# A transformer block on one Trainium2 core: feed-forward product a slot later, window values as a difference, gate product in strips

## The chip, the cores and the metric

The kernel runs on one core of a Trainium2 chip. Its engines run their own instruction streams beside each other: TensorE (PE in the profile, with its weight loads as PEld), VectorE (DVE), ScalarE (ACT), GpSimd (POOL) and SyncE (SP), which here only issues DMAs. They meet through semaphores. The metric is the device time of one execution in microseconds (us).

## The reference

Eight batches of 1024 tokens, 512 wide, go through one block: a modulated layer norm, attention with 16 heads of 32 that adds three parts under a learned gate, a residual, a second modulated layer norm, and a feed-forward part with six routed pairs of rank-16 matrices.

```python
h = _layernorm(x) * (1 + ca) + sa
# attention of h:
q, k, v = _rope(x @ Wq, HD), _rope(x @ Wk, HD), x @ Wv
ck, cv = (blocks of 16 tokens of k and v, weighted by wk_comp, wv_comp)
out_comp = softmax(q ck^T * SCALE, blocks that are over) @ cv
out_sel  = softmax(q k_sel^T * SCALE, causal) @ v_sel       # 2 x 8 tokens of the best 2 blocks
wmask = (cols <= rows) & (cols > rows - WIN)                # WIN = 128
out_win  = softmax(q k^T * SCALE, wmask) @ v
g = softmax(x @ Wg + bg)                                    # 3 gates
out = g0 * out_comp + g1 * out_sel + g2 * out_win
x = x + ga * (out @ Wo + bo)
h = _layernorm(x) * (1 + cb) + sb
# feed-forward of h: top 2 of 6 experts, renormalised weights
x = x + gb * (h @ base_W^T + base_b + (h @ shared_A^T) @ shared_B^T
              + sum_e w_e * (h @ routed_A[e]^T) @ routed_B[e]^T)
```

## The kernel before, in words

A batch is eight tiles of 128 tokens. A token attends in the window part to its own tile and the one before, so a query has 128 keys: for key column j either that of the tile before or its own tile's.

**Stages.** Eight "heads" project batch 0. Then come, for each of seven batches, a first slot, six common slots (`slot`, s = 2 to 7) and a turn; an epilogue (`end_first`, `end_slot`, `last`) finishes batch 7. A slot s does three things at once: attention of tile s of batch b; the output product, residual, second norm, router and feed-forward of tile t = s − 1; and norm, Q, K, V and gate of tile t of batch b + 1. The first slot has attention of tile 1 and the output part of tile 0, and the turn has attention of tile 0 of the next batch and the output part of tile 7, and with them the blocks' compression and the selection.

**What sets the order.** Nothing is scheduled by a program. Each engine's stream is written out by hand in these functions, one list of calls for each engine. Products that end in the two PSUM banks `ps_m` take them in the order of tables (`SLOT_ORDER` and its like, units Q, K, V, QT, KT transposes, G gate, HT, Y output product, H2T, Z router and rank-16 product, F feed-forward, ZT): a unit may begin when the one before it in its bank is read out (`m_free_at`), and its reader waits for `m_full`. Window scores are in `ps_s`, transposed probabilities in `ps_t`, attention values in `ps_o`.

**Precision.** Long products are three fp32r products: hi x hi, lo x hi, hi x lo (L558 to L560 for Q, K, V; L729, L730, L738 for the output; L773, L774, L782 for the feed-forward). Short ones are plain fp32: the gate (`gate_logits`, L579: four chunks of 128x128 tokens as weights against 3 columns), the rank-16 product down (L755) and up (`feed_up`, L790, weights 113 rows).

**Window probabilities.** Scores (L647), VectorE's merge of the two tiles' scores into 128 columns by the mask `later` and the maximum (L1791, L1796), ScalarE's exponentials and normalisation (L1182, L1192), TensorE's transposition of four heads into `ps_t` (L660), two masked copies by VectorE (`split_probs`): `pT_prev` (L1817) for the keys of the tile before, `pT_own` (L1819) for the tile's own keys; the two masks complement each other. Then the values (`window_values`, L685): 16 matmuls in four 32-column strips, `pT_prev` x `v_s[t-1]` and `pT_own` x `v_s[t]`. For tile 0 eight bf16 matmuls with zero open the bank (L695), and only `pT_own` counts.

**Compressed and selected part.** Scores L636, VectorE L1828 to L1856, transposition L679, ScalarE copies it to `pT_cs` (L1219), values L715. The value rows are the tile `csv`; when few blocks are seen, several heads' products run in different rows of TensorE, and so `csv` is replicated by DMA at the start of a batch's first slot: `cv_two` (two copies of 64 rows, L463) and `cv_four` (four of 32 rows, L465), used for tiles 2 and 3, and 0 and 1.

**Other lines that are named.** Residual and norm statistics on VectorE: L1866, L1869, L1718. Rope of Q or K on VectorE (L1758, L1763), then its sum on GpSimd (L1462). The final sum of the block on VectorE (`final`, L1920, L1922), and the store of `xc` by ScalarE's queue. SyncE loads the rows of `x` and the three gate rows `gbc` of a batch in the turn.

## Time and profile before

| | us |
|---|---|
| three runs, median (lowest, highest) | 2219.99 (2219.48, 2226.52) |
| the profiled execution | 2229.21 |
| its span | 2227.3 |
| TensorE busy in it | 2023.9 (91%) |
| VectorE busy | 1793.5 (81%) |
| ScalarE busy | 1327.9 (60%) |
| GpSimd busy | 878.8 (39%) |
| mean granted TensorE clock | 0.967 of full |

The page gives these and the shares of forty slices. Below it, the table of stretches gives each engine's busy time in a stretch, the rows in order of time give each group's start and length with, in brackets, how long the engine was idle before it and which event ended that. Matmul lengths overlap in these rows; the distance between two starts is what a group costs.

### The profile page before, as it was taken

What the parts mean: (1) busy time and instruction counts of PE and PEld (TensorE: products, weight loads), DVE (VectorE), ACT (ScalarE), POOL (GpSimd) and SP (SyncE); (2) the same over time, 40 slices, a digit from 0 to 9 for tenths busy, and PEclk for the clock granted to TensorE, in tenths of its full rate; (3) what the DMA queues carried; (4) which work ended last, traced back from release to release, by engine and by line L of the source; (5) the groups of instructions that cost most, each with busy time, mean ns of one, the idle gap of its engine ahead of it and who ended that gap; (6) DMA issues with size and microseconds to landing.
All of it is one profiled execution on the core that took longest, in us unless ns stands there. A gap on an engine that the chain in (4) does not pass through costs nothing.

```text
span 2227.3 us, 49222 instructions
## 1 busy us (share of the span) xinstructions
PE 2023.9 (91%) x18028; PEld 1465.2 (66%) x18028; DVE 1793.5 (81%) x4806; ACT 1327.9 (60%) x4658; POOL 878.8 (39%) x843
## 2 busy tenths in 40 slices
PE   6988999899999999989999999999999999987876
PEld 3656667666676766667666666766766676665554
DVE  4668888878987888878897788878898788886775
ACT  2346666556665666655666566655666566655654
POOL 1534444334442444334443344434444344432232
PEclk9999999999999999989999999999999999997888
DMA  6210100101011010110001001010001100010000
GB/s 215 63 44 20 30 25 29 44 25 30 20 34 44 20 30 25 33 40 25 25 25 53 15 30 30 30 39 25 29 20 34 44 25 25 29 32 23 20 20 20
DMA packets 43537, 77.56 MB, mean 35 GB/s; under 512 B 7314, under 2 KB 7314, under 8 KB 43299
## 3 DMA queue, kind: packets, MB, share of 16 engines
q1 hardware_dynamic: 32034, 56.85, 8.9%
q10 hardware_dynamic: 11264, 17.57, 2.1%
q8 instruction: 145, 2.38, 0.4%
q14 instruction: 94, 0.76, 0.1%
HBM read 53.38 MB, written 16.83 MB: 32 GB/s over the span
## 4 chain that ended last, share of the span: by engine, by line
PE 51%; DVE 34%; ACT 6%; issue 5%; POOL 2%; DMA 1%; SPq 1%; DVEq 0%; ACTq 0%; POOLq 0%
DVE ps_s L1791 6%; PE ps_o L685 5%; PE ps_t L660 5%; DVE wmax L1796 4%; PE ps_o L715 4%; PE ps_m L558 3%; PE ps_m L560 3%; PE ps_m L559 3%; PE ps_s L679 3%; PE ps_m L755 3%; PE ps_m L773 3%; PE ps_m L774 3%; PE ps_m L782 3%; PE ps_s L636 3%; PE ps_m L790 2%
## 5 line engine op out<-in xcount | busy, mean ns | idle before, releaser
L1182 ACT ACTIVATE pw<-ps_s,wmax 128x128 f32<-128x128 f32 x1024 | 359.3, 380 | 229.6 <-DVE wmax L1796 227.8
L558 PE MATMUL ps_m<-w_hi,h_hi 128*128 128x512 f32 x768 | 340.8, 444 | 8.6 <-DVE h_lo L1927 4.8
L1192 ACT ACTIVATE pw<-pw,wden 128x128 f32<-128x128 f32 x1024 | 313.7, 400 | 30.5 <-DVE wden L1806 30.5
L560 PE MATMUL ps_m<-w_hi,h_lo 128*128 128x512 f32 x768 | 303.2, 395 | 0.0
L559 PE MATMUL ps_m<-w_lo,h_hi 128*128 128x512 f32 x768 | 302.4, 394 | 0.0
L1182 ACT ACTIVATION_READ_ACCUMULATOR pw<-ps_s,wmax 128x1 f32 x1024 | 225.5, 220 | 0.0
L1817 DVE COPY_PREDICATED pT<-keep_prev,ps_t 128x512 f32<-128x512 uint32 x224 | 166.0, 741 | 68.9 <-PE ps_t L660 68.4
L1478 POOL TENSOR_TENSOR css<-css,cden 128x256 f32<-128x256 f32 (+7 forms) x128 | 123.1, 982 | 207.0 <-DVE cden L1856 207.0
L558 PEld LDWEIGHTS ps_m<-w_hi,h_hi 128*128 128x128 f32 x768 | 145.3, 189 | 71.7 <-issue 44.3
L1819 DVE COPY_PREDICATED pT<-keep_own,ps_t 128x512 f32<-128x512 uint32 x256 | 185.3, 724 | 1.0 <-issue 0.3
L685 PE MATMUL ps_o<-pT,v_s 128*32 128x128 f32 x3840 | 168.3, 283 | 13.8 <-DVE pT L1817 8.9
L660 PE MATMUL ps_t<-cst,pw 128*128 128x128 f32 x1024 | 168.3, 290 | 11.4 <-ACT pw L1192 10.4
L647 PE MATMUL ps_s<-kT,qT 32*128 32x256 f32 (+1 forms) x2048 | 144.0, 396 | 29.2 <-ACT pw L1182 21.3
L559 PEld LDWEIGHTS ps_m<-w_lo,h_hi 128*128 128x128 f32 x768 | 145.8, 190 | 34.4 <-issue 11.8
L1505 POOL TENSOR_TENSOR h_lo<-hT,h_hi 128x512 fp32r<-128x512 f32 x57 | 72.8, 1277 | 242.2 <-ACT h_hi L1144 242.2
L560 PEld LDWEIGHTS ps_m<-w_hi,h_lo 128*128 128x128 f32 x768 | 145.1, 189 | 33.8
L1796 DVE TENSOR_REDUCE wmax<-ps_s 128x4 f32<-128x512 f32 x256 | 163.9, 681 | 0.0
L660 PEld LDWEIGHTS ps_t<-cst,pw 128*128 128x128 f32 x1024 | 122.4, 148 | 53.5 <-issue 44.0
L1828 DVE TENSOR_TENSOR css<-ps_s,csmask 128x384 f32<-128x384 f32 (+3 forms) x64 | 65.5, 1024 | 109.9 <-PE ps_s L636 109.7
L1791 DVE COPY_PREDICATED ps_s<-later,ps_s 128x512 f32<-128x512 uint32 x224 | 144.1, 688 | 5.7 <-PE ps_s L647 5.5
L1470 POOL TENSOR_TENSOR css<-css,cm 128x256 f32<-128x256 f32 (+7 forms) x128 | 111.1, 889 | 88.5 <-DVE cm L1841 86.5
L685 PEld LDWEIGHTS ps_o<-pT,v_s 128*32 128x32 f32 x3840 | 93.5, 110 | 79.6 <-issue 44.1
(213 smaller groups left out, 4791.4 us busy)
## 6 DMA issues: line engine op xcount, KB each, us to landing
xa<-x_in SPq DMA_DIRECT2D x65, 256.0 KB, 2.7
xc<-x_in SPq DMA_DIRECT2D x64, 256.0 KB, 2.7
out<-xc ACTq DMA_DIRECT2D x64, 256.0 KB, 2.0
gbc<-gate_rows SPq DMA_DIRECT2D x24, 256.0 KB, 3.4
pw<-wmod_in SPq DMA_DIRECT2D x3, 1024.0 KB, 8.2
pT<-wmod_in SPq DMA_DIRECT2D x3, 1024.0 KB, 7.2
qT<-wqkv_in SPq DMA_DIRECT2D x2, 1024.0 KB, 13.6
cv_two<-csv SPq DMA_DIRECT2D x16, 128.0 KB, 3.1
```

Of the source, the lines that this page charges most:

```text
L558: pe_.matmul(ps[:], h_hi[:, c, :], w_hi[:, col, c, :], start=(c == 0), stop=False)
L559: pe_.matmul(ps[:], h_hi[:, c, :], w_lo[:, col, c, :], start=False, stop=False)
L560: mm = pe_.matmul(ps[:], h_lo[:, c, :], w_hi[:, col, c, :], start=False, stop=(c == NC - 1))
L647: mm = pe_.matmul(ps_s[:, j, (i + 1) * 2 * P - n:(i + 1) * 2 * P], qT[rows, c, t * P:(t + 1) * P], kT[rows, c, k0:k0 + n], start=True, sto ...
L660: mm = pe_.transpose(ps_t[:, j, :], pw[:, head_column(half, j, i), :], ident)
L685: mm = pe_.matmul(ps_o[HD * j:HD * j + HD, c, :], src[0:rows, cols], probs[0:rows, j, :], start=start, stop=stop, skip_group_check=True)
L1182: ins = act.activation(pw[:, hw, :], ps_w[:, j, i, 1, :], ACT.Exp, bias=wmax[:, hw:hw + 1], accum_out=wden[:, 0, hw:hw + 1])
L1192: act.activation(pw[:, hw, :], pw[:, hw, :], ACT.Copy, scale=wden[:, 2, hw:hw + 1]).then_inc(wn_ok, 1)
L1791: dve.copy_predicated(own, later[:].unsqueeze(1).unsqueeze(1).broadcast_to([P, 2, 2, P]), former).then_inc(merged, 1)
L1796: dve.tensor_reduce(wmax[:, h0:h0 + 4].rearrange("p (j i) -> p j i", j=2), ps_w[:, 2 * p:2 * p + 2, :, 1, :], AX.X, ALU.max, negate=True). ...
L1817: dve.copy_predicated(pT_prev[:, g % 2], keep_prev[:].unsqueeze(1).broadcast_to([P, 4, P]), ps_t[:]).then_inc(tw_done, 1)
L1819: dve.copy_predicated(pT_own[:, g % 2], keep_own[:].unsqueeze(1).broadcast_to([P, 4, P]), ps_t[:]).then_inc(tw_done, 1 if t else 2)
```

## The change

1. **Feed-forward a slot later.** The product F of a tile, its rank-16 part (ZT, `feed_up`), `final` and the store move into the slot of the next tile, in front of the output product. The first call of all has nothing to do and only passes the semaphores on; `last` has the units F2 and ZT2 for the last tile. The residual `x1` has two buffers. SyncE loads gate row 1 in slot 2, once F of the tile before has used the old one.
2. **Value difference.** ScalarE copies the whole of `ps_t` to `pT_all`, and this copy frees `ps_t`. VectorE's masked copy to `pT_own` reads `pT_all`, and none is made to a `pT_prev`. GpSimd computes `vd = v_s[t] - v_s[t-1]`, and the values are `pT_all` x `v_s[t-1]` + `pT_own` x `vd`. Tile 0 uses `pT_all` x `v_s[0]` alone, without zero matmuls.
3. **Gate strips.** Four matmuls with 128x32 weights (`wg_w`) against `hT` in four column strips, a copy by ScalarE (`gs`), and one matmul that adds the four and gives 3 columns (unit G2).
4. **Split rank product.** `feed_up` is three fp32r matmuls; VectorE computes the low part of `zT` (`lower_z`).
5. **One replicated tile.** `cv_rep` takes the place of `cv_two` and `cv_four`: four 32-row copies first, the two 64-row ones in slot 2.
6. **Other order.** All engines' lists and the bank tables are written anew.

```diff
-SLOT_ORDER = [("Y", 1), ("Q", 0), ("K", 1), ("QT", 0), ("G", 0), ("H2T", 0), ("Z", 0), ("KT", 1),
-              ("F", 0), ("ZT", 1), ("V", 1), ("HT", 0)]
+SLOT_ORDER = [("F", 0), ("ZT", 1), ("Y", 1), ("Q", 0), ("K", 1), ("QT", 0), ("G", 0), ("G2", 0),
+              ("H2T", 0), ("V", 1), ("Z", 0), ("KT", 0), ("HT", 0)]
...
+            def spread_values(b, parts):
+                if parts == 4:
+                    sp.wait_ge(cv_done, b + 2)
+                else:
+                    sp.wait_ge(pvc_done, values_through(rounds_before(NT * b + 1)) + 1)
+                w = P // parts
+                for k in range(parts):
+                    sp.dma_start(cv_rep[w * k:w * k + w, :], csv[0:w, :]).then_inc(d_cv, 16)
...
-                for c in chunks:
-                    mm = pe_.matmul(ps[:, 0:3], hT[:, c, :], wg_s[:, c, :], start=(c == 0), stop=(c == NC - 1))
+                for c in range(NC):
+                    mm = pe_.matmul(ps[32 * c:32 * c + 32, 0:P], wg_w[:, c, :], hT[:, c, :], start=True, stop=True,
+                                    skip_group_check=True)
+                mm.then_inc(full, 1)
+
+            def gate_sum(seg, b, t):
+                pe_.wait_ge(*m_free_at(seg, b, "G2", t))
+                ps, full = m_target(seg, b, "G2", t)
+                pe_.wait_ge(*m_done_at(seg, b, "G", t))
+                pe_.matmul(ps[:, 0:3], gs[:, :], strip_sum[:, :], start=True, stop=True).then_inc(full, 1)
...
-                    if t == 0:
-                        pe_.matmul(ps_o[:], ident_b[:, :], zero_b[:].unsqueeze(1).broadcast_to([P, NC, P]),
-                                   start=True, stop=False, skip_group_check=True)
+                pe_.wait_ge(ta_done, n + 2)
+                mm = add_values(g, v_s[:, max(t - 1, 0), :], pT_all[:, g % 2], t > 0 or g == 0, False)
                 if t:
-                    pe_.wait_ge(tw_done, 2 * n + 2)
-                    add_values(g, v_s[:, t - 1, :], pT_prev[:, g % 2], True, False)
-                pe_.wait_ge(tw_done, 2 * n + 3)
-                add_values(g, v_s[:, t, :], pT_own[:, g % 2], False, False).then_inc(pvw_done, 1)
+                    if g == 0:
+                        pe_.wait_ge(vd_ok, (NT - 1) * b + t + 1)
+                    pe_.wait_ge(to_done, split_before(b, t, g) + 2)
+                    mm = add_values(g, vd[:], pT_own[:, g % 2], False, False)
+                mm.then_inc(pvw_done, 1)
...
-                pe_.matmul(ps[:], zT[:, :], wb_s[:, :], start=False, stop=True).then_inc(full, 1)
+                pe_.matmul(ps[:], zT_hi[:, :], wb_hi[:, :], start=False, stop=False)
+                pe_.matmul(ps[:], zT_hi[:, :], wb_lo[:, :], start=False, stop=False)
+                pe_.matmul(ps[:], zT_lo[:, :], wb_hi[:, :], start=False, stop=True).then_inc(full, 1)
...
+            def value_change(b, t):
+
+                gp.wait_ge(pvw_done, 4 * (NT * b + t) + 1)
+                gp.tensor_tensor(vd[:], v_s[:, t, :], v_s[:, t - 1, :], ALU.subtract).then_inc(vd_ok, 1)
...
                 n = 4 * (NT * b + t) + g
-                dve.wait_ge(tw_full, n + 2)
-                if t > 0 or g > 1:
-                    dve.wait_ge(pvw_done, n)
+                dve.wait_ge(ta_done, n + 2)
+                dve.wait_ge(pvw_done, n)
                 dve.sem_inc(seen, 1)
-                if t:
-                    dve.copy_predicated(pT_prev[:, g % 2], keep_prev[:].unsqueeze(1).broadcast_to([P, 4, P]), ps_t[:]
-                                        ).then_inc(tw_done, 1)
-                dve.copy_predicated(pT_own[:, g % 2], keep_own[:].unsqueeze(1).broadcast_to([P, 4, P]), ps_t[:]
-                                    ).then_inc(tw_done, 1 if t else 2)
+                dve.copy_predicated(pT_own[:, g % 2], keep_own[:].unsqueeze(1).broadcast_to([P, 4, P]), pT_all[:, g % 2]
+                                    ).then_inc(to_done, 1)
...
-                dve.wait_ge(f_ok, T + 1)
-                dve.tensor_tensor(x1[:], ps[:], gbc[:, 0, :], ALU.mult).then_inc(done, 1)
+                if T > 1:
+                    dve.wait_ge(f_ok, T)
+                x1_ = x1[:, T % 2, :]
+                dve.tensor_tensor(x1_, ps[:], gbc[:, 0, :], ALU.mult).then_inc(done, 1)
```

How the instructions stand now. TensorE, common slot, where the feed-forward product of a tile ends. Before, this is late in the slot, between transposed probabilities (`ps_t`) and the V product (L558, L559):

```order
L782 MATMUL ps_m<-wbt_hi,h_lo 128x512 x3
L762 MATMUL ps_m<-cst,zr 113x128
L782 MATMUL ps_m<-wbt_hi,h_lo 128x512
L660 MATMUL ps_t<-cst,pw 128x128 x4
L790 MATMUL ps_m<-wb_s,zT 128x512
L558 MATMUL ps_m<-w_hi,h_hi 128x512
L559 MATMUL ps_m<-w_lo,h_hi 128x512
```

After, it is early in the slot, behind the first window scores (L674) and in front of the output product (L756):

```order
L674 MATMUL ps_s<-kT,qT 128x256 x8
L794 MATMUL ps_m<-cst,zr 113x128
L821 MATMUL ps_m<-wbt_hi,h_lo 128x512 x4
L834 MATMUL ps_m<-wb_hi,zT_hi 128x512
L835 MATMUL ps_m<-wb_lo,zT_hi 128x512
L836 MATMUL ps_m<-wb_hi,zT_lo 128x512
L756 MATMUL ps_m<-wo_hi,aT_hi 128x512
```

The whole feed-forward product moved from behind the K product to the front, and the V product has lost it as its neighbour.

VectorE, middle of the same slot, around the gate's sum (`gl`) and rope K (`kr`, `rbf`). Before:

```order
L1779 TENSOR_TENSOR gl<-ps_m,bg_s 128x3
L1781 TENSOR_REDUCE gl<-gl 128x1
L1817 COPY_PREDICATED pT<-keep_prev,ps_t 128x512
L1819 COPY_PREDICATED pT<-keep_own,ps_t 128x512
L1758 TENSOR_TENSOR kr<-ps_m,cst 128x512
L1763 TENSOR_TENSOR rbf<-ps_m,cst 128x256 x2
L1817 COPY_PREDICATED pT<-keep_prev,ps_t 128x512
L1819 COPY_PREDICATED pT<-keep_own,ps_t 128x512
```

After (L1985 to L2012 are the same operations under new lines):

```order
L1985 TENSOR_TENSOR gl<-ps_m,bg_s 128x3
L1987 TENSOR_REDUCE gl<-gl 128x1
L1964 TENSOR_TENSOR kr<-ps_m,cst 128x512
L1969 TENSOR_TENSOR rbf<-ps_m,cst 128x256 x2
L2021 COPY_PREDICATED pT<-keep_own,pT 128x512 x2
L2010 RECIPROCAL wden<-wden 128x8
L2012 TENSOR_SCALAR wden<-wden,gates 128x8
```

Rope K moved ahead of the masked copies, of which two are left in this piece.

TensorE, first slot, where the values of the compressed part of tile 0 stand. Before, right behind Q, K and one transposition of `css`:

```order
L647 MATMUL ps_s<-kT,qT 128x256 x8
L558 MATMUL ps_m<-w_hi,h_hi 128x512
L559 MATMUL ps_m<-w_lo,h_hi 128x512
L560 MATMUL ps_m<-w_hi,h_lo 128x512
L679 MATMUL ps_t<-cst,css 128x128 x4
L715 MATMUL ps_o<-pT,cv_four 32x128 x16
L569 MATMUL ps_m<-cst,ra 128x128 x4
L660 MATMUL ps_t<-cst,pw 128x128 x4
L636 MATMUL ps_s<-csk,qT 128x32 x16
```

After, with the feed-forward product of the last tile also ahead of them in the slot:

```order
L687 MATMUL ps_t<-cst,pw 128x128 x4
L742 MATMUL ps_o<-pT,cv_rep 32x128 x8
L600 MATMUL ps_m<-hT,wg_w 32x128 x4
L742 MATMUL ps_o<-pT,cv_rep 32x128 x4
L663 MATMUL ps_s<-csk,qT 128x32 x16
L742 MATMUL ps_o<-pT,cv_rep 32x128 x4
L608 MATMUL ps_m<-strip_sum,gs 128x3
L591 MATMUL ps_m<-cst,ra 128x128 x4
```

The values moved behind 15 rows of feed-forward work and a transposition of window probabilities, and stand apart in three pieces.

## Rows read from the trace of the kernel before

**Rows 1.** the page's first part: busy time, share and instructions of each engine
```profile
PE 2023.9 (91%) x18028; PEld 1465.2 (66%) x18028; DVE 1793.5 (81%) x4806; ACT 1327.9 (60%) x4658; POOL 878.8 (39%) x843
```

**Rows 2.** stretches: us, then PE, PEld, DVE, ACT, POOL busy (instructions), clock, DMA, GB/s
```profile
523.01:554.26 31.25, 29.64 (x279) 21.84 (x279) 27.19 (x72) 20.20 (x74) 13.93 (x13) 1.00 0.10 27
649.52:682.53 33.01, 31.76 (x248) 21.23 (x245) 25.58 (x83) 19.00 (x70) 9.90 (x11) 1.00 0.10 30
682.53:720.07 37.54, 34.02 (x315) 25.27 (x311) 29.30 (x82) 20.44 (x72) 12.07 (x14) 0.91 0.19 52
695.10:701.90 6.80, 6.80 (x50) 5.73 (x48) 5.34 (x12) 4.89 (x14) 4.01 (x5) 0.50 0.01 2
1995.76:2227.30 231.54, 174.67 (x1674) 122.16 (x1674) 161.30 (x424) 124.32 (x456) 62.45 (x64) 0.84 0.07 23
2066.84:2092.60 25.76, 20.78 (x224) 13.95 (x225) 21.26 (x55) 16.30 (x63) 7.61 (x8) 0.93 0.06 22
```

**Rows 3.** PE in order of time, common slot: start, us, engine, line, operation
```profile
535.05 1.05 PE L579 MATMUL ps_m<-wg_s,hT 128*128 128x3 f32 x8 [0.25 <-ACT qT L1154]
535.96 0.49 PE L558 MATMUL ps_m<-w_hi,h_hi 128*128 128x512 f32 x1
536.29 0.40 PE L559 MATMUL ps_m<-w_lo,h_hi 128*128 128x512 f32 x1
536.52 0.40 PE L560 MATMUL ps_m<-w_hi,h_lo 128*128 128x512 f32 x1
...
541.41 0.65 PE L685 MATMUL ps_o<-pT,v_s 128*32 128x128 f32 x16
541.98 0.66 PE L679 MATMUL ps_s<-cst,css 128*128 128x128 f32 x4
...
546.69 1.02 PE L790 MATMUL ps_m<-wb_s,zT 113*128 113x512 f32 x2
...
547.79 0.40 PE L559 MATMUL ps_m<-w_lo,h_hi 128*128 128x512 f32 x1
```

**Rows 4.** DVE in order of time, the same common slot
```profile
527.98 0.68 DVE L1866 TENSOR_TENSOR x<-ps_m,gbc 128x512 f32<-128x512 f32 x1
...
532.13 1.28 DVE L1791 COPY_PREDICATED ps_s<-later,ps_s 128x512 f32<-128x512 uint32 x2
...
537.37 0.74 DVE L1817 COPY_PREDICATED pT<-keep_prev,ps_t 128x512 f32<-128x512 uint32 x1
...
538.63 0.68 DVE L1758 TENSOR_TENSOR kr<-ps_m,cst 128x512 f32<-128x512 f32 x1
...
539.98 0.75 DVE L1817 COPY_PREDICATED pT<-keep_prev,ps_t 128x512 f32<-128x512 uint32 x1
```

**Rows 5.** groups of instructions by line and form: busy us, mean ns, idle before
```profile
L1817 DVE COPY_PREDICATED pT<-keep_prev,ps_t 128x512 f32<-128x512 uint32 x224 | 166.0, 741 | 68.9 <-PE ps_t L660 68.4
...
L1462 POOL TENSOR_TENSOR ra<-ra,rbf 128x512 f32<-128x512 f32 x64 | 82.3, 1286 | 109.1 <-DVE rbf L1763 109.1
...
L1219 ACT ACTIVATE pT<-ps_s 128x512 f32<-128x512 f32 x72 | 42.9, 595 | 34.4 <-PE ps_s L679 34.2
```

**Rows 6.** one line's instructions (L1869): ns min/median/max, first and last start
```profile
L1869 DVE TENSOR_TENSOR x<-x,xc x64: 691/692/1165, 179.7 to 2210.5; 128x512 f32<-128x512 f32 x64
```

**Rows 7.** PE in order of time, first slot of batch 1
```profile
693.56 1.08 PE L715 MATMUL ps_o<-pT,cv_four 24*32 24x128 f32 x32 [1.90 <-DMA cv_four<-csv]
...
704.73 0.66 PE L569 MATMUL ps_m<-cst,kr 128*128 128x128 f32 x4 [0.78 <-DVE x L1866]
```

**Rows 8.** SyncE's DMA queue in the same first slot
```profile
687.96 1.14 SPq L463 DMA_DIRECT2D cv_two<-csv  x2
689.14 2.89 SPq L465 DMA_DIRECT2D cv_four<-csv  x4
```

**Rows 9.** PE in order of time, an end slot of the epilogue
```profile
2074.36 2.09 PE L647 MATMUL ps_s<-kT,qT 32*128 32x256 f32 x16 [3.29 <-ACT pw L1182]
...
2079.68 1.12 PE L755 MATMUL ps_m<-wa_s,h2T 128*128 128x118 f32 x8 [1.69 <-ACT h2T L1134]
```

791 lines of the change are left out of this document (450 added, 341 removed).

## The prediction

> **What bounds the kernel now.** I read the page's busy times first, then the table of stretches, then TensorE's rows in order of time. TensorE is busy 2023.9 of 2227.3 us [rows 1], and the time is that of three kinds of stretch [rows 2]. The stretch from 523.01 us is one of the 42 common slots (six in each of seven batches): 31.25 us, TensorE busy 29.64, VectorE 27.19, so TensorE has 1.6 us idle and VectorE 4.1. That from 649.52 is one of the seven turns, 33.01 us with 31.76 busy. That from 682.53 is one of the seven first slots, 37.54 us, with a granted clock of 0.91; its piece from 695.10 ran for 6.80 us at 0.50, which is the lower of TensorE's levels (1.2 of 2.4 GHz). The epilogue from 1995.76 is other in kind: 231.54 us with 174.67 busy and a clock of 0.84, where TensorE waits for a chain through the other engines. Heads and prologue make the rest.
>
> So in the slots a microsecond counts only if it is TensorE's own work or one of its 1.6 us of waits, and what frees VectorE pays only where TensorE waits for VectorE. In the first slot there is more to get: 37.54 − 34.02 = 3.5 us without TensorE, among them waits of 1.90 us for the copy cv_four and of 0.78 behind the residual [rows 7], and half clock behind the first.
>
> **TensorE's own work in a slot.** The gate's fp32 matmuls start at 535.05 and the next K product at 535.96 [rows 3]: 0.91 us for four 128x128 weights against 3 columns. In their place stand four 128x32 weights against 128 columns, in four column strips, and one 128x128 weight against 3 columns. Nearest rows: eight value matmuls in four strips, 541.41 to 541.98, 0.57 us, so four are 0.28 if they overlap as those do; the sum matmul is a quarter of 0.91, 0.23, with 0.02 for its start: 0.53, a gain of 0.38. If strips did not overlap, four would take about 1.0, and the sum another 0.23: a loss of 0.3. I take 0.53, since the shape is the one in the row.
>
> The rank product starts at 546.69 and the second matmul of V at 547.79, 1.10 us of which 0.33 are V's first: 0.77 in fp32. Three fp32r matmuls of 512 columns go at 0.23 each, as 536.29 does behind 535.96 when it is warm: 0.69, a gain of 0.08 (bounds 0.69 and 0.85). Behind an fp32 matmul the first fp32r one takes 0.33 instead of 0.23 [rows 3]; one such place goes: 0.10. The sum is 29.64 − 0.38 − 0.08 − 0.10 = 29.1 us, the floor of a slot.
>
> **What waits instead.** The value difference takes the 0.74 us copy to pT_prev away four times a slot from VectorE and gives ScalarE four copies of 0.595 [rows 5]; ScalarE has 31.25 − 20.20 = 11 us spare in a slot, so these are covered. GpSimd gets one 128x512 op of 1.286 [rows 5] with 31.25 − 13.93 = 17 us spare. lower_z is about 0.2 us on VectorE, and TensorE's next use of that bank lies behind. VectorE then has some 25 us of work in 31. But that freed time lies in one place: the copies stood between the gate's sum and rope K and after it [rows 4], and now follow rope K. The second order excerpt shows it.
>
> The cycle that I expect to end last: all of the output product is in its bank 8.8 us into the slot (scores of compressed keys 1.1, F 1.9 and 0.9, window scores 1.1, ZT 0.3, rank product 0.7, output 2.8). VectorE's residual starts 0.3 later. From it to the second merge of the window scores are 532.13 − 527.98 = 4.15 us, from that merge to the end of the gate's sum 537.37 − 532.13 = 5.24, and rope K takes 539.98 − 538.63 = 1.35 [rows 4]. Its bank is the one that the V product wants: V starts 0.3 + 4.15 + 5.24 + 1.35 = 11.0 us after the output. TensorE has some 9.4 us of work between them (Q 2.8, K 2.8, window scores 1.1, transposes of Q, h2 and two of probabilities 1.7, gate 0.5, switches 0.5), so it waits 1.6 to 1.7 us, and from V to the end of the slot 11.0 more follow. Period: 8.8 + 11.0 + 11.0 = 30.8 to 30.9. **Slots: −0.35 × 42 = −15 us.** Before, V stood after the feed-forward product, and rope K was long over (V's second matmul at 547.79 [rows 3], rope K's next at 539.98). So most of the 0.56 of work and of the 1.6 of old waits turns into one new wait.
>
> **Turns.** They win 0.38 + 0.08 + 0.10, and the transpose of K waits about as before for rope K behind the residual: −0.6 × 7 = **−4**.
>
> **First slots.** Here three copies of the compressed values decide. Now the two for cv_two go out at 687.96 ahead of the four for cv_four at 689.14, and these take 2.89 us [rows 8]; TensorE reaches its 32 matmuls at 691.67 and stands until 693.56 [rows 7]. Afterwards the four go first, and the 15 matmuls of the feed-forward of tile 7 are done before TensorE comes there, some 3.5 us later. So the wait goes twice over, and with it what I take to be the cause of the half clock: the 1.90 us stand in front of every such stretch. 6.80 us at half clock hold 3.4 us of lost time. The other 1.6 of the 3.5 us idle also go, because feed-forward rows stand between. With new stalls a little under a slot's, 1.3: 37.54 − 3.5 − 3.4 − 0.56 + 1.3 = 31.4. **−6.1 × 7 = −43.** SyncE's later loads (gate row 1, the two 64-row copies) are needed only from slot 3 on, and copies like them take 1.1 to 2.9 us [rows 8]: nothing.
>
> The Trainium skill, "TensorE: Matmul & The Clock Gate", section "HAM oscillation — how this bites in real kernels", says that TensorE which waits between bursts is throttled and starts the next burst cold. By that rule too the half clock goes when the wait goes. What the rule leaves open is rival A.
>
> **Epilogue.** 25.76 us for an end slot, busy 20.78 [rows 2], with waits of 3.29 for ScalarE's exponentials and 1.69 for the transposed h2 in front of the rank-16 product [rows 9]. The second is covered now by the feed-forward of the tile before (3.5 us of work that depends on nothing new), less 0.34 in new waits; the first stays, and the clock with it. −1.35 × 6 = −8. end_first loses its 4 us wait for the copied values in part, −3; the last stretch has one feed-forward more and waits less, ±0. **−11.**
>
> **Prologue and heads.** Gate 0.38 × 7 less 1.5 to build the strips' weights: **−1.**
>
> Sum −15 − 4 − 43 − 11 − 1 = −74. From the profiled execution (2229.2 us, span 2227.3) that is 2155; the median of the runs is 9.2 lower, 2146. I take the middle, rounded up: **2152**.
>
> **The price of the own copy** has no row of its own. It is a masked copy of 128x512 from SBUF to SBUF; masked copies that read PSUM take 0.74 [rows 5] or 1.28 for two [rows 4]; an addition with two SBUF inputs takes 0.691 at least, 0.692 in the middle and 1.165 at most [rows 6]. I take 0.74, nearest in kind. At 0.74 to 1.165 its four copies a slot lie behind rope K and before the next slot's scores, and VectorE keeps 6 down to 4 us idle.
>
> **Rivals.**
> A. The wait or the half clock in the first slots survives, since something else stands there (the exponentials, the gate rows' loads). For: 1.90 us is short for such a loss, and later clock drops in the epilogue stand behind waits of other length. Price: 3.4 × 7 = 24: 2176. Chance 0.15.
> B. VectorE gets to rope K sooner than I add up (its 5.24 us hold two pieces that could go earlier), so that the wait for V is gone. TensorE's floor is 29.1; with 0.8 of the old waits left a slot takes 29.9, −1.0 × 42 = −42: 2110. Chance 0.09.
> E. Strips do not overlap. (0.38 + 0.3) × 64 = +44: 2196. Chance 0.04.
> D. VectorE's chain is longer: final and lower_z now stand ahead of the residual. If they delay it by 1.7 us in each slot, 42 × 1.7 = +71 and the slots lose what all else gains: 2223. For: final is two ops of 0.7 that did not stand there. Against: the residual waits for an output that is itself 2.8 us further down. Chance 0.05.
> C. **Slower.** The own copy reads two SBUF tensors, and so may stand in the way of GpSimd. What the trace shows is that an addition with two SBUF inputs, 0.692 in the middle, once took 1.165 [rows 6]. If each of 4 copies waits for a whole GpSimd operation of 128x512, 1.286 us [rows 5], that is 5.1 a slot; VectorE's slack on its own path is about 1.8, so 3.3 × 42 = +139: 2291. It decides from a mean of 1.15 us a copy, and eats the whole gain at about 1.5. Against: median and minimum of those rows are equal. Chance 0.09.
>
> The Trainium skill, "SBUF — State Buffer", section "SBUF: two separate sides", says that a VectorE operation with two SBUF inputs and a GpSimd operation that reads SBUF share one port pair as an exclusive lock, so that the later one blocks fully. That speaks for C as a mechanism; by it each copy that meets GpSimd costs the rest of that operation, and the trace agrees only for the few longest of the 64 additions.
>
> **Numbers.** Forecast with its own range 2120 to 2175: 0.58. A 0.15, B 0.09, C 0.09, D 0.05, E 0.04. The range from just under B to 2212 (E with a little of A) leaves out C, D and the tails. A measurement of this kernel tells 0.3%, about 7 us, from no change. Faster: all but C and D, 0.86; same: D, 0.05; slower: C, 0.09.
>
> **What would show it.** In the changed profile: slots of 30.9 us with one wait of TensorE of 1.5 to 2 us in front of V for rope K (none: B; more than 3: D); own copies of 0.74 (over 1.15: C); strips and sum within 0.55 (0.9 or more: E); first slots of 31 to 32 us at a clock of 1.00 with no wait for the copied values (a piece at 0.50: A); end slots 1.3 shorter with a clock still under 0.95. The prediction is most wrong if VectorE's path is other than through rope K, since slots and first slots then move together, or if the epilogue's clock changes.

## The result

The changed kernel takes 2091.84 us (median of 4 runs, 2089.25 to 2092.61) against 2222.97 us for the one before: a ratio of 0.9408, with a 95% interval of 0.9387 to 0.9429. It is 131 us faster where 71 had been forecast, and lies below the range. Its profiled execution has a span of 2090.4 us, 136.9 less than before.

The busy line and the granted clock of the page after, to be read against [rows 1]:

```profile
PE 1948.7 (93%) x18212; PEld 1422.7 (68%) x18212; DVE 1736.9 (83%) x4614; ACT 1458.5 (70%) x4979; POOL 971.4 (46%) x900
...
PEclk9999999999999999999999999999999999998999
```

The same kinds of stretch as in [rows 2], but without its half-clock piece: a common slot, a turn, a first slot, the epilogue, an end slot. The columns are those of [rows 2].

```profile
498.24:528.41 30.17, 29.11 (x286) 21.63 (x283) 26.31 (x70) 22.22 (x77) 15.45 (x15) 1.00 0.10 27
620.57:653.31 32.74, 31.11 (x251) 21.38 (x247) 23.93 (x82) 23.21 (x80) 8.79 (x9) 1.00 0.13 40
653.31:684.87 31.56, 30.70 (x319) 22.18 (x315) 25.98 (x76) 21.34 (x75) 15.69 (x17) 1.00 0.15 37
1886.34:2090.40 204.06, 162.78 (x1676) 111.87 (x1672) 150.82 (x406) 134.69 (x479) 76.47 (x72) 0.92 0.08 26
1943.90:1968.70 24.80, 20.68 (x225) 14.06 (x226) 19.34 (x52) 18.01 (x67) 9.37 (x9) 0.93 0.07 23
```

To see where the time went I cut both traces at the starts of TensorE's first instruction of every slot and added up by kind (the epilogue's row in [rows 2] begins 2.7 us ahead of its first instruction, at 1995.76 instead of 1998.5):

| kind | before | after | difference | forecast |
|---|---|---|---|---|
| 42 common slots | 1336.6 | 1276.1 | −60.5 | −15 |
| 7 turns | 230.9 | 229.2 | −1.7 | −4 |
| 7 first slots | 272.3 | 221.9 | −50.4 | −43 |
| epilogue | 228.8 | 204.1 | −24.7 | −11 |
| heads and prologue | 158.7 | 159.2 | +0.5 | −1 |
| span | 2227.3 | 2090.4 | −136.9 | −74 |

Two terms are wrong: the slots by a factor of four, the epilogue by more than two. The slot's mechanism is visible in TensorE's rows of slot 4 of batch 1, in order of time:

```profile
503.57 0.42 PE L834 MATMUL ps_m<-wb_hi,zT_hi 113*128 113x512 f32 x1
...
504.30 0.40 PE L756 MATMUL ps_m<-wo_hi,aT_hi 128*128 128x512 f32 x1
...
513.00 0.63 PE L591 MATMUL ps_m<-cst,ra 128*128 128x128 f32 x4 [0.28 <-POOL ra L1632]
...
514.69 0.43 PE L600 MATMUL ps_m<-hT,wg_w 128*32 128x128 f32 x8
515.05 0.50 PE L580 MATMUL ps_m<-w_hi,h_hi 128*128 128x512 f32 x1
...
516.53 0.63 PE L774 MATMUL ps_m<-cst,xc 128*128 128x128 f32 x4 [0.40 <-DVE gl L1985]
...
517.97 0.50 PE L580 MATMUL ps_m<-w_hi,h_hi 128*128 128x512 f32 x1 [0.38 <-DVE rbf L1969]
```

V (517.97) does wait for rope K, as forecast, but 0.38 us and not 1.7; 0.40 more stands in front of the transposed h2, for the gate's sum, and 0.28 in front of Q's transposition, for GpSimd. I had named neither of these two. Over all 42 slots the waits for the gate's sum and for rope K are 20.8 and 15.8 us:

```profile
PE ps_m L774 <- DVE gl L1985: 20.8, 42, 0.8
...
PE ps_m L580 <- DVE rbf L1969: 15.8, 42, 0.4
```

VectorE's rows of the same slot are the path (residual, second merge of window scores, rope K, own copy), as [rows 4] before:

```profile
507.29 0.69 DVE L2070 TENSOR_TENSOR x<-ps_m,gbc 128x512 f32<-128x512 f32 x1
...
511.39 1.28 DVE L1997 COPY_PREDICATED ps_s<-later,ps_s 128x512 f32<-128x512 uint32 x2
...
516.56 0.69 DVE L1964 TENSOR_TENSOR kr<-ps_m,cst 128x512 f32<-128x512 f32 x1
...
517.84 0.84 DVE L2021 COPY_PREDICATED pT<-keep_own,pT 128x512 f32<-128x512 uint32 x1
```

The chain of work that ended last runs through the same rows in this slot:

```profile
506.32 0.94 PE ps_m L765 x4
...
507.29 0.70 DVE x L2070
...
517.17 0.76 DVE rbf L1969 x2
...
517.97 0.50 PE ps_m L580
```

The residual starts 0.04 us after the profile's end of the last matmul of the output product. From it to the end of rope K VectorE never stands idle for more than 0.2 us in any of the 42 slots, and V follows 0.05 us later. The output has little margin as the start of this chain: VectorE comes free from the final sum of the tile before only 0.14 us ahead of its residual, and in slot 7 the residual starts 0.3 us after the output is complete.

### The profile page after: what moved, and what is told of

It reads as the page before. It is cut to its first block, busy times and chain, and to the rows that moved or that the text cites. A ratio compares the mean times of both kernels' runs of the same rounds, so it can differ in the third digit from the quotient of the medians.

```text
span 2090.4 us, 50389 instructions
## 1 busy us (share of the span) xinstructions
PE 1948.7 (93%) x18212; PEld 1422.7 (68%) x18212; DVE 1736.9 (83%) x4614; ACT 1458.5 (70%) x4979; POOL 971.4 (46%) x900
## 4 chain that ended last, share of the span: by engine, by line
PE 55%; DVE 29%; issue 6%; ACT 5%; POOL 4%; DMA 0%; SPq 0%; DVEq 0%; ACTq 0%; POOLq 0%
PE ps_o L712 5%; PE ps_m L580 4%; PE ps_m L582 3%; PE ps_m L581 3%; DVE ps_s L1997 3%; PE ps_t L687 3%; PE ps_o L742 3%; DVE rbf L1969 3%; PE ps_m L782 3%; PE ps_s L663 3%; DVE wmax L2002 3%; PE ps_s L706 3%; PE ps_m L809 3%; PE ps_s L674 3%; DVE cden L2051 2%
## 5 line engine op out<-in xcount | busy, mean ns | idle before, releaser
L580 PE MATMUL ps_m<-w_hi,h_hi 128*128 128x512 f32 x768 | 336.6, 438 | 18.0 <-DVE rbf L1969 15.8
L2021 DVE COPY_PREDICATED pT<-keep_own,pT 128x512 f32<-128x512 uint32 x224 | 199.1, 895 | 58.4 <-ACT pT L1358 56.4
L1632 POOL TENSOR_TENSOR ra<-ra,rbf 128x512 f32<-128x512 f32 x64 | 82.4, 1288 | 302.5 <-DVE rbf L1969 302.5
L580 PEld LDWEIGHTS ps_m<-w_hi,h_hi 128*128 128x128 f32 x768 | 146.1, 190 | 82.7 <-issue 33.6
L1358 ACT ACTIVATE pT<-ps_t 128x512 f32<-128x512 f32 x256 | 156.8, 613 | 49.7 <-PE ps_t L687 46.7
L674 PE MATMUL ps_s<-kT,qT 32*128 32x256 f32 (+1 forms) x2048 | 142.8, 393 | 32.5 <-ACT pw L1272 28.7
L687 PE MATMUL ps_t<-cst,pw 128*128 128x128 f32 x1024 | 159.5, 279 | 4.3 <-ACT pT L1358 2.2
L1997 DVE COPY_PREDICATED ps_s<-later,ps_s 128x512 f32<-128x512 uint32 x224 | 143.9, 688 | 10.4 <-PE ps_s L674 10.2
L1673 POOL TENSOR_TENSOR h_lo<-h2T,h_hi 128x512 fp32r<-128x512 f32 x64 | 97.9, 1530 | 104.3 <-ACT h_hi L1324 104.3
L674 PEld LDWEIGHTS ps_s<-kT,qT 32*128 32x128 f32 x2048 | 90.8, 186 | 81.6 <-ACT pw L1272 37.5
L1261 ACT ACTIVATE css<-css 128x384 f32<-128x384 f32 (+3 forms) x64 | 57.9, 904 | 116.2 <-POOL css L1640 116.2
```

Of the source, the lines that this page charges most:

```text
L580: pe_.matmul(ps[:], h_hi[:, c, :], w_hi[:, col, c, :], start=(c == 0), stop=False)
L674: mm = pe_.matmul(ps_s[:, j, (i + 1) * 2 * P - n:(i + 1) * 2 * P], qT[rows, c, t * P:(t + 1) * P], kT[rows, c, k0:k0 + n], start=True, sto ...
L687: mm = pe_.transpose(ps_t[:, j, :], pw[:, head_column(half, j, i), :], ident)
L1358: act.activation(pT_all[:, g % 2], ps_t[:], ACT.Copy).then_inc(ta_done, 1)
L1997: dve.copy_predicated(own, later[:].unsqueeze(1).unsqueeze(1).broadcast_to([P, 2, 2, P]), former).then_inc(merged, 1)
L2021: dve.copy_predicated(pT_own[:, g % 2], keep_own[:].unsqueeze(1).broadcast_to([P, 4, P]), pT_all[:, g % 2]).then_inc(to_done, 1)
```

## The experiments

Each kernel is the changed one or the one before with one edit. The table gives the medians and, from the profiled execution of each, the mean of the 42 common slots and of the 7 first slots, and the length of the epilogue. All are from cuts like those above.

| kernel | median us | ratio to before (95%) | slot | first slot | epilogue |
|---|---|---|---|---|---|
| before | 2222.97 | 1 | 31.82 | 38.9 | 228.8 |
| after | 2091.84 | 0.941 (0.939–0.943) | 30.38 | 31.7 | 204.1 |
| after, old gate | 2099.95 | 0.946 (0.944–0.948) | 30.41 | 33.0 | 204.7 |
| after, pad on the path | 2117.0 | 0.954 (0.952–0.955) | 31.00 | 31.8 | 204.2 |
| after, pad in the slack | 2094.69 | 0.944 (0.942–0.945) | 30.42 | 31.8 | 205.5 |
| after, three pads | 2199.18 | 0.990 (0.987–0.993) | 32.94 | 31.4 | 204.5 |
| after, no value difference | 2328.59 | 1.049 (1.047–1.051) | 34.63 | 39.1 | 211.7 |
| the same, copies earlier | 2301.63 | 1.035 (1.032–1.038) | 33.73 | 40.5 | 212.3 |
| after, own copy from PSUM | 2268.33 | 1.022 (1.018–1.026) | 33.38 | 37.5 | 212.1 |
| before, value difference alone | 2264.72 | 1.022 (1.016–1.027) | 32.03 | 42.7 | 229.8 |
| the same, second placing | 2258.78 | 1.016 (1.015–1.018) | 32.01 | 42.3 | 229.9 |
| before, four copies first | 2218.28 | 0.999 (0.996–1.002) | 31.92 | 37.4 | 225.6 |
| after, rope K early | 2278.61 | 1.025 (1.022–1.029) | 34.82 | 31.7 | 205.2 |
| after, path short | 2128.61 | 0.958 (0.955–0.961) | 31.25 | 31.7 | 205.1 |
| after, path short, second | 2121.09 | 0.955 (0.954–0.957) | 31.04 | 31.7 | 205.8 |
| after, end slots: feed first | 2116.52 | 0.953 (0.950–0.956) | 30.38 | 31.9 | 228.8 |
| after, end slots: old second wait | 2108.06 | 0.949 (0.948–0.951) | 30.38 | 31.9 | 219.8 |

### Is it VectorE's path or TensorE's work that sets the slot?

The old gate product in the changed kernel:

```diff
-                    mm = pe_.matmul(ps[32 * c:32 * c + 32, 0:P], wg_w[:, c, :], hT[:, c, :], start=True, stop=True,
-                                    skip_group_check=True)
+                    mm = pe_.matmul(ps[:, 0:3], hT[:, c, :], wg_s[:, c, :], start=(c == 0), stop=(c == NC - 1))
...
-                pe_.matmul(ps[:, 0:3], gs[:, :], strip_sum[:, :], start=True, stop=True).then_inc(full, 1)
+                pe_.sem_inc(full, 1)
...
-                act.activation(gs[:, :], ps[:, 0:P], ACT.Copy).then_inc(done, 1)
+                act.sem_inc(done, 1)
```

> The changed kernel with the gate product as it was before (four fp32 matmuls with 128x128 weights against 3 columns, 0.91 us instead of 0.36 for the strips and 0.17 for their sum), all else as changed. Theory P, VectorE's path from the residual to rope K sets a common slot: the 0.38 us more of TensorE lie beside that path and come out of its waits (0.25 to 0.81 us in front of the transposed h2, 0.38 in front of V), so the 42 slots lose nothing, and only turns, first slots and heads lose 0.38 each, 21 x 0.38 = 8 us: 2092 to 2104 us. Rival F, TensorE's own work sets the slot: 64 x 0.38 = 24 us: 2116 us.

It took 2099.95 us, 8 more. The slot's window, with TensorE's waits in it:

```profile
499.80:529.89 30.09, 29.27 (x284) 21.99 (x281) 26.21 (x71) 22.05 (x76) 15.46 (x15) 1.00 0.08 29
```

```profile
518.02 0.63 PE L773 MATMUL ps_m<-cst,xc 128*128 128x128 f32 x4 [0.17 <-DVE gl L1984]
...
519.46 0.50 PE L580 MATMUL ps_m<-w_hi,h_hi 128*128 128x512 f32 x1 [0.37 <-DVE rbf L1968]
```

TensorE has more work, its wait for the gate's sum is 0.17 instead of 0.40, and the slot is as long as with the strips (30.41 against 30.38 on average). The gate strips bring nothing in the 42 slots. In the profiled execution the first slots are 8.8 us longer and the turns 1.1: first slots at full clock are 0.6 longer each (32.15 against 31.57), and four of the seven have a granted clock of 0.90 to 0.95 and take 33.4 to 34.0, where in the changed kernel only the first of all is below 1.00. The strips also save less TensorE time than forecast: 29.27 − 29.11 = 0.16 us in this slot and not 0.38. The old product costs 516.90 − 516.09 = 0.81 here, against 0.91 in the kernel before, and the strips' 0.36 are above the 0.28 forecast.

One VectorE operation added on the path, or at the end of the list:

```diff
                 residual(seg, b, t)
                 window_weights(b, s, 0)
+                dve.bn_stats(junk[:], x1[:, (NT * b + t) % 2, :]).then_inc(seen, 1)
                 rope(seg, b, t, "Q")
```

> The changed kernel with one more VectorE operation of about 0.69 us (statistics of a 128x512 tile into an unused tile) in each of the 42 common slots, between the residual and rope Q. Theory P: it lies on the path that sets the slot, 42 x 0.69 = 29 us: 2121 us. Rival F, TensorE's work sets the slot and its waits are only what is left over: under 10 us: 2092 to 2102 us.

> The same operation as in the run with it between residual and rope Q, but at the end of VectorE's list in each common slot, behind the router. Theory P: VectorE has idle time there, and the next slot's path begins only with the output product, so 0 to 5 us: 2092 to 2097 us. Rival V, all VectorE time counts alike: 29 us, as the other place: 2121 us.

On the path it cost 25 us (2117.0): every slot is 0.6 us longer, 31.00 against 30.38. At the end of the list it cost 3 (2094.69), within what two medians can differ, with slots of 30.42. The window with the pad on the path has TensorE busy for the same 29.11 us in a longer slot:

```profile
504.38:535.12 30.74, 29.11 (x286) 21.62 (x282) 26.90 (x71) 22.22 (x77) 15.43 (x15) 1.00 0.08 26
```

Where the 0.6 us appear says how far the pads reach. TensorE's waits for rope K and for the gate's sum stay as they were (16.0 and 20.7 us in 42 places); what grows is its wait for GpSimd's rotated Q, in the changed kernel and with the pad:

```profile
PE ps_m L591 <- POOL ra L1632: 13.6, 42, 0.6
```

```profile
PE ps_m L592 <- POOL ra L1633: 37.1, 42, 1.1
```

The pad stands ahead of rope Q and so lengthens the way to Q's transposition as well as that to V. The pads and the old gate thus show that VectorE's stretch from the residual on is on the path, and that TensorE's own work and the end of VectorE's list are not. That the path goes on to rope K and V is read from the trace above (no gap on VectorE, V 0.05 us behind rope K); a pad between rope Q and rope K was not tried. Together they bear out the forecast's mechanism.

Three such operations:

```diff
+                dve.bn_stats(junk[:, 0:6], x1[:, (NT * b + t) % 2, :]).then_inc(seen, 1)
+                dve.bn_stats(junk[:, 6:12], x1[:, (NT * b + t) % 2, :]).then_inc(seen, 1)
+                dve.bn_stats(junk[:, 12:18], x1[:, (NT * b + t) % 2, :]).then_inc(seen, 1)
                 rope(seg, b, t, "Q")
```

> Three operations of 0.69 us between residual and rope Q instead of the one that cost 25 us. Theory P alone: three times as much, 75 us: 2167 us. Theory W, a wait of TensorE near 3 us in a slot also brings pieces of 3.4 us at half clock (as in the run where the own copy read PSUM, whose slots take 31.9 or 33.5 us): up to 1.7 us more in each of 42 slots, 2185 to 2240 us.

2199.18 us: 107 more, not 75. Two of its windows:

```profile
483.56:516.82 33.26, 30.61 (x287) 22.55 (x283) 27.74 (x73) 22.38 (x77) 14.97 (x15) 0.95 0.08 25
516.82:548.71 31.89, 29.06 (x286) 21.62 (x282) 28.08 (x74) 22.22 (x77) 15.42 (x15) 1.00 0.08 26
```

In these two neighbours TensorE is busy 30.61 and 29.06 us for the same instructions: the longer slot has a mean clock of 0.95, which is one piece of 3.4 us at half clock. 19 of the 42 slots have a clock of 1.00 and 23 have one piece or two. With one pad none had any. So a stall of TensorE costs itself, and here the three pads together brought half clock as well, one pad did not.

### What the value difference gives

The changed kernel without it: VectorE makes both masked copies from PSUM, and TensorE's next transposition waits for both.

```diff
-                dve.wait_ge(ta_done, n + 2)
+                dve.wait_ge(tw_full, n + 2)
...
+                dve.copy_predicated(pT_all[:, g % 2], keep_prev[:].unsqueeze(1).broadcast_to([P, 4, P]), ps_t[:]
+                                    ).then_inc(ta_done, 1)
-                dve.copy_predicated(pT_own[:, g % 2], keep_own[:].unsqueeze(1).broadcast_to([P, 4, P]), pT_all[:, g % 2]
+                dve.copy_predicated(pT_own[:, g % 2], keep_own[:].unsqueeze(1).broadcast_to([P, 4, P]), ps_t[:]
...
+                pe_.wait_ge(to_done, split_before(b, t, g) + 1)
...
-                    mm = add_values(g, vd[:], pT_own[:, g % 2], False, False)
+                    mm = add_values(g, v_s[:, t, :], pT_own[:, g % 2], False, False)
```

> The changed kernel with the window values as before: two masked copies by VectorE from the transposed probabilities (previous tile's and own tile's), values from v[t-1] and v[t], no copy by ScalarE and no difference by GpSimd for tiles 1 to 7. VectorE gets 4 x (2 x 0.74 - 0.895) = 2.3 us more in a slot, all of it behind rope K. Theory P, only the path to rope K counts: VectorE has 3.9 us idle in a slot of 30.17, so most is covered, with up to 0.7 us a slot where it is nearly full (slots 6 and 7): 2095 to 2122 us. Rival V, the time taken off VectorE is what the change gained: 42 x 2.3 = 97 us: 2189 us.

2328.59 us, 237 more than after: outside both expectations. A slot of it, and the wait that makes it long:

```profile
543.34:577.49 34.15, 30.55 (x286) 22.77 (x282) 28.00 (x75) 20.48 (x73) 13.77 (x13) 0.95 0.06 21
```

```profile
PE ps_t L689 <- DVE pT L2023: 169.0, 102, 3.1
```

The slot also has a piece of half clock (0.95). VectorE is busy 28.00 of 34.15 us, so it is not short of time. TensorE waits 169 us for the tile ps_t, because VectorE empties it only after rope K. I had looked at VectorE's idle time and not at who holds the tile. The next run separates the two: the own copy alone reads PSUM again, so VectorE has less to do than in the changed kernel, but ps_t is held until it comes.

```diff
-                dve.copy_predicated(pT_own[:, g % 2], keep_own[:].unsqueeze(1).broadcast_to([P, 4, P]), pT_all[:, g % 2]
+                dve.copy_predicated(pT_own[:, g % 2], keep_own[:].unsqueeze(1).broadcast_to([P, 4, P]), ps_t[:]
...
                 pe_.wait_ge(ta_done, n + 1)
+                pe_.wait_ge(to_done, split_before(b, t, g) + 1)
```

> The changed kernel, but VectorE's masked copy of the own tile's probabilities reads the transposed probabilities in PSUM instead of ScalarE's copy of them, and TensorE's next transposition waits for both copies. VectorE's time falls (0.74 instead of 0.895 us a copy). Theory R, what the value difference gives is that ScalarE frees the PSUM tile at once while VectorE comes to it only after rope K: the tile is again held until VectorE is there, the slots take 33 to 34.5 us as in the run without the value difference, 2220 to 2320 us. Rival V, VectorE's time counts: 4 x 0.15 x 42 = 26 us less, 2066 to 2092 us.

2268.33 us, 176 more than after. Two neighbouring slots of it:

```profile
531.64:563.71 32.07, 29.14 (x286) 21.59 (x282) 25.59 (x71) 22.45 (x77) 15.03 (x14) 1.00 0.07 25
563.71:597.50 33.79, 30.72 (x287) 22.80 (x283) 26.90 (x71) 22.68 (x77) 15.52 (x14) 0.95 0.07 25
```

VectorE is busy 25.59 us in the first, 0.7 less than after, and the slot is 1.9 us longer; the second has a piece of half clock besides. TensorE stands 128.4 us in front of the transpositions into ps_t, in 102 places, as many as in the run before (the profile names no releaser for most of it). With the value difference undone and VectorE's first pair of copies put ahead of rope K:

```diff
                 gates_soft(seg, b, t, Ta, 0)
+                split_probs(b, s, 0)
                 rope(seg, b, t, "K")
-                split_probs(b, s, 0)
                 split_probs(b, s, 1)
```

> The run without the value difference again, but with VectorE's first pair of copies ahead of rope K, as the kernel before had it. Theory R: what made that run slow (34.2 us a slot) is that the PSUM tile was held until VectorE had done rope K, so the slots fall to the changed kernel's 30.2 us plus one pair of copies on the path (1.48): 31.5 to 32 us, 2140 to 2175 us. Rival V, VectorE's total is at fault: as before, 2300 to 2330 us.

2301.63 us. The slots 2 without a half-clock piece (six of seven) take 32.2 to 32.3 us, near the expectation's 32, and those of the first batch, all at a clock of 1.00, up to 33.6; most others have a piece and take 33.8 to 34.7. TensorE still waits 119.7 us for ps_t, since the second pair stands behind rope K. The mechanism (who holds ps_t) held, the size did not: I had left out the clock and the second pair. What this order would do with every pair placed ahead of its reader was not tried.

The other way round, the kernel before with the value difference alone, all orders as they were (ScalarE's four copies a slot put in behind the copy of Q, the transposed h2, the second normalisation and the second copy of the compressed part):

```diff
+            def probs_all(b, t, g):
...
+                act.activation(pT_prev[:, g % 2], ps_t[:], ACT.Copy).then_inc(tw_done, 1)
...
-                    dve.copy_predicated(pT_prev[:, g % 2], keep_prev[:].unsqueeze(1).broadcast_to([P, 4, P]), ps_t[:]
-                                        ).then_inc(tw_done, 1)
+                    dve.copy_predicated(pT_own[:, g % 2], keep_own[:].unsqueeze(1).broadcast_to([P, 4, P]),
+                                        pT_prev[:, g % 2]).then_inc(to_done, 1)
```

> The kernel before with the value difference alone (ScalarE copies the transposed probabilities whole, VectorE makes the own-tile copy from that, GpSimd computes the difference of the value tiles), all orders as before. Theory R: in the old order VectorE makes its copies ahead of rope K and nobody waits long for the PSUM tile (TensorE idles 1.6 to 2.4 us a slot, for four different things), so of the 2.3 us that VectorE saves a slot 0 to 0.5 arrives: 2198 to 2222 us. Rival V, the time taken off VectorE is the gain: 42 x 2.3 = 97 us, 2125 us.

2264.72 us, 42 slower than before. In the common slots nothing was gained:

```profile
537.61:568.87 31.26, 29.92 (x284) 21.66 (x280) 25.06 (x68) 21.99 (x76) 15.75 (x15) 1.00 0.09 27
```

VectorE's 27.19 us of [rows 2] have become 25.06, and the slot is 31.26 instead of 31.25. Three quarters of the loss, 27 of 37 us of the span, are in the first slots (42.7 against 38.9), and 9 in the common slots. VectorE waits for ScalarE's copy, here over the whole run:

```profile
DVE pT L1856 <- ACT pT L1260: 164.4, 123, 5.8
```

A second placing of one of these copies,

```diff
                 copy_qT(seg, b, t)
                 probs_all(b, 1, 0)
+                probs_all(b, 1, 1)
                 probs_copy(b, 0, 2)
                 window_norm(b, 1, 1)
-                probs_all(b, 1, 1)
```

> The kernel before with the value difference alone again, with ScalarE's copy of the second group of probabilities in the first slot ahead of its normalisation instead of behind (VectorE waited 3.2 us for it). Theory R: the common slots stay where they were (31.3 to 33.2 us, no gain), and the first slots give back what that place cost, 2 to 4 us each: 2235 to 2250 us, level with or just above the kernel before. Rival: the loss in the first slots has another cause: 2260 to 2268 us.

gave 2258.78 us, with the slots at 32.01 and the first slots at 42.3: hardly anything back. Whether a better placing of ScalarE's copies would give the first slots' loss back is not shown; that the slots don't gain was seen twice.

So the value difference by itself, in the two placings tried, is worth nothing, and the new order without it is worse than the kernel before by 5%. It pays because ScalarE empties ps_t at once, and that allows VectorE to do rope K first.

### First slots and the clock

The kernel before with the four 32-row copies first:

```diff
-                for k in range(2):
-                    sp.dma_start(cv_two[64 * k:64 * k + 64, :], csv[0:64, :]).then_inc(d_cv, 16)
                 for k in range(4):
-                    sp.dma_start(cv_four[32 * k:32 * k + 32, :], csv[0:32, :]).then_inc(d_cv, 16)
+                    sp.dma_start(cv_four[32 * k:32 * k + 32, :], csv[0:32, :]).then_inc(d_cv4, 16)
+                for k in range(2):
+                    sp.dma_start(cv_two[64 * k:64 * k + 64, :], csv[0:64, :]).then_inc(d_cv, 16)
...
-                    pe_.wait_ge(d_cv, 16 * REPLICAS * (b + 1))
+                    pe_.wait_ge(d_cv4, 16 * 4 * (b + 1))
```

> The kernel before with one thing changed: the four 32-row copies of the compressed values are issued ahead of the two 64-row copies, and the first slot waits for those four alone. They are issued 1.18 us earlier (at the place of 687.96 instead of 689.14), so TensorE's wait of 1.90 us falls to about 0.7. Theory W, the half clock in the first slots follows from that wait: it goes too, a first slot takes 38.9 (mean) down to 33 us: 7 x 5.9 = 41, 2178 us. Rival N, the half clock has another cause: 7 x 1.2 = 8 us, 2211 us.

2218.28 us, ratio 0.9985 (0.9955 to 1.0015): no difference. TensorE's rows of the same first slot as in [rows 7]:

```profile
689.05 1.08 PE L718 MATMUL ps_o<-pT,cv_four 24*32 24x128 f32 x32 [0.84 <-ACT pT L1222]
692.08 1.09 PE L637 MATMUL ps_s<-csk,qT 32*128 32x32 f32 x32 [0.92 <-ACT pw L1185]
699.31 0.66 PE L570 MATMUL ps_m<-cst,kr 128*128 128x128 f32 x4 [2.00 <-DVE x L1870]
```

The DMA is awaited no longer in the seven first slots, but 2.00 us for the residual take its place (0.78 before). Four of seven first slots had no half clock and took 35.9 us, three had it and took 38.0 to 40.0. So neither expectation: the half clock doesn't hang on the wait for the DMA alone, and without it the first slot's other waits remain. In the changed kernel only a wait of 0.61 us is left in this first slot (in front of the transposed h2), and the half clock is gone with the others: it is 31.56 us long at 1.00. Six of the seven are at 1.00; the first of all has 0.95 and 32.2 us. That the feed-forward work in between is what covers these waits is read from the two orders, not tried by itself, and it is not enough: the changed kernel without the value difference has neither the wait for the DMA nor that for the residual in a first slot, but two for ps_t, of 2.83 and 3.04 us, a clock of 0.91 and 39.1 us. The first slots' gain needs both parts of the change.

### Could the path be made shorter?

Three tries on the changed kernel. Rope K straight behind the second maximum, V ahead of the transposed h2:

```diff
                 window_max(b, s, 1)
+                rope(seg, b, t, "K")
                 cs_factor(b, s)
                 ln_scale(x1[:, t % 2, :], mvc, vec, xc[:, t % 2, :], lnc, lncp, NT * b + t)
                 gates_soft(seg, b, t, Ta, 0)
-                rope(seg, b, t, "K")
```

> The changed kernel with rope K on VectorE straight behind the second maximum of the window scores in the common slots (ahead of the compressed part's factors, 2.06 us, the norm's scaling and the gate's sum), and on TensorE the first two V chunks and one transposition of probabilities ahead of the transposed h2. Theory P: TensorE's two waits in a slot (0.25 to 0.81 for the gate's sum, 0.38 for rope K) go, 0.6 to 1.1 us a slot, unless ScalarE is late with h2: 42 x 0.7 = 29 us, 2062 us. Rival F, the slot is at TensorE's floor by now: under 8 us, 2084 to 2092 us.

2278.61 us, 187 slower. K is not complete by then, and VectorE stands still where it may not. From slot 3 on every slot also has a granted clock of 0.90 to 0.95:

```profile
DVE kr L1964 <- PE ps_m L582: 92.7, 43, 2.2
```

Second, K completed one step sooner, rope K between the sums and the rest of the compressed part's factors (VectorE's list, then TensorE's):

```diff
-                cs_factor(b, s)
+                cs_factor(b, s, 0)
                 ln_scale(x1[:, t % 2, :], mvc, vec, xc[:, t % 2, :], lnc, lncp, NT * b + t)
+                rope(seg, b, t, "K")
+                cs_factor(b, s, 1)
                 gates_soft(seg, b, t, Ta, 0)
-                rope(seg, b, t, "K")
...
-                project(seg, b, t, "K", 1, [2])
+                project(seg, b, t, "K", 1, [2, 3])
                 transpose_window(b, s, 0)
                 gate_logits(seg, b, t)
-                project(seg, b, t, "K", 1, [3])
+                transpose_window(b, s, 1)
+                project(seg, b, t, "V", 2, [0])
                 gate_sum(seg, b, t)
+                project(seg, b, t, "V", 2, [1])
                 transpose_h2(seg, b, t)
-                transpose_window(b, s, 1)
-                project(seg, b, t, "V", 2, [0, 1])
```

> The changed kernel with VectorE's path from the residual to V made shorter in the common slots: rope K now stands behind the two sums for the compressed part's factors and the norm's scaling, and the rest of the factors and the gate's sum behind it; on TensorE K is finished one step sooner and V starts ahead of the gate's sum and the transposed h2. Theory P: V can start 16.7 - 7.3 = 9.4 instead of 10.7 us behind the residual, so 0.5 to 0.8 of the two waits (0.25 to 0.81 and 0.38 us) goes: 42 x 0.65 = 27 us less, 2065 us (2058 to 2078). Rival L: h2 and the router come about 1 us later and TensorE waits there instead: 2085 to 2110 us.

2128.61 us, 37 slower. The V wait went, and TensorE waited 47.1 us for GpSimd, which had got the factors later:

```profile
PE ps_s L706 <- POOL css L1648: 47.1, 37, 1.8
```

Third, rope K directly behind the factors:

```diff
                 cs_factor(b, s)
+                rope(seg, b, t, "K")
                 ln_scale(x1[:, t % 2, :], mvc, vec, xc[:, t % 2, :], lnc, lncp, NT * b + t)
                 gates_soft(seg, b, t, Ta, 0)
-                rope(seg, b, t, "K")
...
                 gate_sum(seg, b, t)
-                transpose_h2(seg, b, t)
                 transpose_window(b, s, 1)
                 project(seg, b, t, "V", 2, [0, 1])
+                transpose_h2(seg, b, t)
```

> The changed kernel with rope K directly behind the factors of the compressed part (its K product is complete at that moment), the norm's scaling and the gate's sum behind it, and on TensorE V's first two chunks ahead of the transposed h2. Unlike in the two orders tried before, neither K nor the factors are touched, so nobody there waits longer. Theory P, VectorE's path from residual to V sets the slot: it is 0.7 us shorter, of which 0.3 to 0.5 arrive (V must follow the transposition of probabilities): 42 x 0.4 = 17 us less, 2075 us (2068 to 2084). Rival L, h2 0.7 us later costs as much at its end: 2090 to 2105 us.

2121.09 us, 29 slower. From the residual (510.19) to V (520.34) are now 10.15 us instead of 10.68, so the path did get shorter:

```profile
520.34 0.50 PE L580 MATMUL ps_m<-w_hi,h_hi 128*128 128x512 f32 x1 [0.83 <-DVE rbf L1969]
524.81 0.42 PE L742 MATMUL ps_o<-pT,cv_rep 56*32 56x128 f32 x8 [0.65 <-ACT pT L1313]
```

But V, now ahead of h2, stands longer in front of rope K, and behind it TensorE waits 0.65 us for ScalarE, whose list has h2 ahead of the copy of the compressed part. Theory P's numbers fail here, its rival's hold in kind: around this path several others are only tenths of a microsecond shorter, and the order that was changed to is a balance of them. None of the three beats it, so no run shows a gain from a shorter path, only losses from a longer one.

### The epilogue

Feed-forward products ahead of the second window scores, to cover TensorE's wait for the exponentials:

```diff
+                feed(seg, b, t, [0, 1, 2, 3])
                 window_scores(b, s, 1)
-                feed(seg, b, t, [0])
                 transpose_window(b, s, 0)
-                feed(seg, b, t, [1, 2])
                 transpose_window(b, s, 1)
-                feed(seg, b, t, [3])
```

> The changed kernel with the feed-forward's high products ahead of the second window scores in the six end slots of the epilogue, where TensorE waits 3.1 to 3.4 us for ScalarE's exponentials. Theory E: 1.9 us of the wait is covered, and with the wait the half-clock piece of 3.4 us behind it goes: 6 x (1.9 + 1.7) = 22 us less at most, 2070 to 2084 us. Rival: the chain through VectorE and ScalarE sets these 25 us, the wait only moves to the transpositions behind: 2086 to 2094 us.

2116.52 us, 25 slower, the epilogue 228.8 instead of 204.1 us. The wait for the exponentials became a longer one, for the low part of zT, whose bank the feed-forward product takes:

```profile
1956.04 0.79 PE L809 MATMUL ps_m<-wbt_hi,h_hi 128*128 128x512 f32 x1 [3.92 <-DVE zT_lo L2198]
```

The old second wait put back:

```diff
                 transpose_h2(seg, b, t)
+                lora_down(seg, b, t)
                 feed_low(seg, b, t, [0, 1, 2, 3])
                 window_values(b, s, 0)
                 feed_up(seg, b, t)
-                lora_down(seg, b, t)
```

> The changed kernel with the rank-16 product down straight behind the transposed h2 in the six end slots, as the kernel before had it, so that TensorE waits 1.7 us there for ScalarE beside the 3.2 us for the exponentials. Theory W, the second wait is what gave the kernel before pieces of 10.2 us at half clock in every other end slot (3.4 in each now): 6 x 1.35 = 8 us of wait, and up to 6 x 1.7 = 10 us of clock: 2102 to 2112 us. Rival N, the clock doesn't depend on it: 2092 to 2100 us.

2108.06 us, 16 slower, inside the expectation of theory W, but in other shares. The epilogue of this run, and its waits for the transposed h2:

```profile
1885.98:2105.82 219.84, 166.71 (x1676) 116.66 (x1672) 147.99 (x406) 135.34 (x479) 76.31 (x72) 0.90 0.08 24
```

```profile
PE ps_m L782 <- ACT h2T L1224: 16.4, 8, 2.7
```

In the changed kernel that line reads 2.0 us in 5 places. TensorE's idle time in the epilogue is 219.84 − 166.71 = 53.1 us against 41.3, and its busy time 166.71 against 162.78: about 12 of the 16 us are waiting, since the wait is up to 2.7 us long here and not 1.7, and 4 are the clock. The half-clock pieces of the epilogue add up to 44 us instead of 30.6 (clock 0.90 against 0.92) and are far from the 74.8 of the kernel before. One of its two waits, put back alone, thus brings back its own length and little of the clock.

## Why the prediction was wrong

**What held.** The floor: TensorE busy 29.11 us in slot 4, forecast 29.1. That is in part luck: the strips gave 0.16 of the 0.53 and not 0.38, and the rest gave 0.37 and not 0.18. The rank product, 504.30 − 503.57 = 0.73 us, forecast 0.69. The mechanism of the slot, shown by the pads, the old gate and the rows from the residual to V. In slot 4 the first two pieces of its cycle: the residual starts 507.29 − 498.24 = 9.05 us into the slot (forecast 8.8 + 0.3), and V 10.68 behind it (4.15 + 5.24 + 1.35 = 10.74). The first slots: 31.56 us at a clock of 1.00 (31.4), no wait for the compressed values. The turns gave 1.7 of the 4 us forecast. Rivals A, C, D and E did not come: half clock stays only in the first of the seven first slots, the mean own copy is 0.895 us, under the 1.15 from which it decides, and the four strips take 515.05 − 514.69 = 0.36 us together. Of D there is a trace in slot 7, where VectorE reaches its residual 0.3 us late.

**What failed first: the piece behind V, and the size of the new wait.** I put V to the end of the slot at 11.0 us, without a sum behind it; it is 528.41 − 517.97 = 10.44. With 0.1 from the two pieces before it, that makes slot 4 0.7 us shorter than forecast (30.17 against 30.85): 42 × 0.7 = 29 us of the 45 that the term is short. The total of TensorE's work was right (8.8 + 9.4 + 11.0 = 29.2 against 29.11), its division was not: between the output and V stand 10.88 − 1.06 = 9.8 us of work (Q starts at 507.09, and 1.06 are the three waits) and not 9.4. Work ahead of V fills the wait for VectorE, work behind V adds to the period. So the waits in that piece are 1.06 us together instead of 1.6 to 1.7, and only 0.38 of them are in front of V. An error of 2% in a sum of three pieces was more than the whole forecast gain of 0.35 us a slot; the bounds should have said so, and they reached only to rival B, whose 29.9 us was the nearer number with a chance of 0.09.

**What failed second: one slot for all.** Slot 4 was 31.25 us, but the 42 slots of before averaged 31.82 (slots 6 and 7 took 32.3 and 32.7, and three early slots had half clock). After, they average 30.38 against slot 4's 30.17. The gain in slot 4 is 1.08, the mean gain 1.44: 0.36 × 42 = 15 us.

**What failed third: the epilogue's clock.** The forecast counted the covered wait (1.35 a slot) and said that the clock stays, since the wait for the exponentials stays. That wait stayed (3.24 us at 1951.41), but before, end slots with both waits had pieces of 10.2 and of 3.4 us at half clock, mostly by turns, and now, with one wait, each has 3.4:

```profile
2046.80:2057.00 10.20, 7.91 (x35) 6.48 (x28) 5.66 (x13) 7.11 (x29) 2.68 (x3) 0.50 0.01 2
```

```profile
1952.10:1955.50 3.40, 3.40 (x20) 2.29 (x13) 2.47 (x4) 2.89 (x10) 1.18 (x1) 0.50 0.00 0
```

The first is of the kernel before, the second of the changed one. The half-clock pieces of the whole epilogue fell from 74.8 to 30.6 us. TensorE's idle time fell from 56.9 to 41.3 us, 15.6 where 11 had been forecast, and its busy time from 171.98 to 162.78, by 9.2 us, although one more feed-forward product stands in it. These 9.2 had been put at nothing: that much at least is the clock's. What exactly halved the pieces stays open: the run with the second wait put back has 44 us of them, so that wait is a part of the cause and not all of it.

**The first slots** were 7 us short for the same reason: the one I used (37.54) was among the lightest of before; two took 41 us with 10.2 us at half clock.

**Which part gave the gain** is not what its size on an engine says. The gate strips save 0.16 us of TensorE in slot 4 and bring nothing there; the value difference brings nothing alone, and its absence costs 237 us in this order, half clock included. What the feed-forward part's move brings by itself was not tried, as all bank tables hang on it; that it covers waits in the first slots and end slots is read from the traces.

## What to carry to other kernels

Before pricing an edit by the engine time it saves, ask which buffer it frees earlier and for whom: here a copy moved to an engine with time to spare was worth 237 us in one order and nothing in the other. When the slot is a cycle of three pieces, a forecast of its gain is only as good as the sum of all three, so give it the error of that sum as a range and take all slots, not one. Ask of each microsecond of work on which side of the wait it lies: ahead of it it costs nothing, behind it it costs itself. Where the edit gives or takes TensorE a wait of a microsecond or more in a repeated stretch, price a piece of half clock with it (here 1.5 us a slot), in the range if not in the sum.

## What the runs showed of the hardware

VectorE's own copy from SBUF and GpSimd do hinder each other, as rival C had it, only below the 1.15 us from which it would decide. The own copy took 0.712 to 1.501 us, 0.745 in the middle; GpSimd's low part of h2 took 1.512 in the middle, where the same operation of the kernel before took 1.286:

```profile
L2021 DVE COPY_PREDICATED pT<-keep_own,pT x224: 712/745/1501, 177.6 to 2067.8; 128x512 f32<-128x512 uint32 x112
```

```profile
L1673 POOL TENSOR_TENSOR h_lo<-h2T,h_hi x64: 1269/1512/1748, 194.1 to 2080.6; 128x512 fp32r<-128x512 f32 x64
```

```profile
L1500 POOL TENSOR_TENSOR h_lo<-h2T,h_hi x64: 1262/1286/1297, 187.8 to 2216.8; 128x512 fp32r<-128x512 f32 x64
```

The last is of the kernel before. The run whose own copy reads PSUM, with all orders as in the changed kernel, has neither spread:

```profile
L2022 DVE COPY_PREDICATED pT<-keep_own,ps_t x224: 710/730/759, 175.5 to 2240.1; 128x512 f32<-128x512 uint32 x112
```

```profile
L1674 POOL TENSOR_TENSOR h_lo<-h2T,h_hi x64: 1267/1277/1284, 197.5 to 2252.9; 128x512 fp32r<-128x512 f32 x64
```

Sorted by what runs beside them, the changed kernel's own copies take 1.11 us on average where a GpSimd operation overlaps (93 of 224) and 0.74 where none does; in the run that reads PSUM the 79 with such an overlap take 0.72. GpSimd's low part of h2 takes 1.50 to 1.75 us with a copy beside it (42 of 64) and 1.27 to 1.28 without. The source in SBUF is thus what makes the two slow each other. The Trainium skill, "SBUF — State Buffer", section "SBUF: two separate sides", says that the two engines share one port pair as an exclusive lock, in which the later one blocks. These rows agree in kind. What it costs in this kernel is small: the copies lie behind rope K, where a whole operation of 0.69 us a slot cost 3 us in all.

The same slot of the same kernel comes in two lengths. With the own copy from PSUM, slot 4 takes 32.1 us at a mean clock of 1.00 in one batch and 33.5 to 33.7 at 0.95 in the six others. So a series of pads is not linear (25 us for one, 107 for three).
